# Five engines, ten hand-written orders: every table of a fused attention and expert kernel written anew

## The reference

```python
x = x + cluster_attention(_layernorm(x), ...)   # 8 batches of 512 rows
x = x + experts(_layernorm(x), ...)
x = x + landmark_attention(_layernorm(x), ...)
x = x + experts(_layernorm(x), ...)
```

```python
KV = K @ V
V = 0.25 * V @ (13.0 * I - KV @ (15.0 * I - KV @ (7.0 * I - KV)))
```

## Time and profile before

| | us |
|---|---|
| median of 3 runs | 1121.43 (1120.27 to 1126.33) |
| span of the profiled execution | 1121.9 |
| PE busy | 933.2 (83%) |
| VectorE busy | 831.1 (74%) |
| ScalarE busy | 641.6 (57%) |
| GpSimd busy | 472.3 (42%) |
| mean granted clock of TensorE | 0.925 of full speed |

### The profile page before, as it was taken

How to read it: one execution, slowest core, us unless ns; L and a number is a source line. 1 busy time by engine, 2 the same in 40 slices (tenths; PEclk the granted TensorE clock), 3 DMA queues, 4 the chain that set the end, 5 groups by cost and what they waited for, 6 DMA issues and landing times. The chain is left out here.

```text
span 1121.9 us, 37263 instructions
## 1 busy us (share of the span) xinstructions
PE 933.2 (83%) x15213; PEld 666.9 (59%) x15213; DVE 831.1 (74%) x2089; ACT 641.6 (57%) x1387; POOL 472.3 (42%) x443
## 2 busy tenths in 40 slices
PE   7899989998989888677888986597689989772898
PEld 5567667675766665456566665454466666552653
DVE  3899899888557996567776687878487898685556
ACT  2456656782664574456667585356376776382630
POOL 2355345227356630445524156512543454446421
PEclk8899989999999999888999998689789999895999
DMA  9700000002321100120101101100311110102533
GB/s 319 254 3 3 4 2 3 3 3 95 115 72 58 31 8 13 38 68 12 49 21 52 41 12 35 30 29 2 102 42 50 39 46 20 49 26 90 160 105 99
DMA packets 51079, 61.71 MB, mean 55 GB/s; under 512 B 5601, under 2 KB 46177, under 8 KB 50913
## 3 DMA queue, kind: packets, MB, share of 16 engines
q1 hardware_dynamic: 43584, 42.51, 11.8%
q0 software_dynamic: 5760, 15.74, 4.4%
q10 hardware_dynamic: 1568, 1.09, 0.3%
HBM read 29.70 MB, written 29.62 MB: 53 GB/s over the span
## 5 line engine op out<-in xcount | busy, mean ns | idle before, releaser
L764 POOL TENSOR_TENSOR a_pr<-a_pr,a_smax 128x512 f32<-128x512 f32 x128 | 133.3, 1042 | 177.5 <-DVE a_smax L877 168.0
L1267 POOL TENSOR_TENSOR b_tm<-b_aw,b_sq 128x640 f32<-128x640 f32 (+1 forms) x48 | 65.4, 1362 | 148.9 <-ACT b_sq L1505 143.5
L871 DVE TENSOR_TENSOR a_pr<-a_bank,a_mask 128x512 f32<-128x512 f32 x128 | 82.8, 682 | 42.0 <-PE a_bank L1066 34.7
L963 ACT ACTIVATE a_pr<-a_pr 128x512 f32<-128x512 f32 x128 | 78.6, 630 | 51.9 <-POOL a_pr L764 44.1
L1247 POOL TENSOR_TENSOR b_pa<-b_pa,b_amax 128x512 f32<-128x512 f32 x64 | 67.1, 1048 | 70.3 <-ACT b_pa L1470 61.8
L969 ACT ACTIVATE a_pT<-a_bank 128x512 f32<-128x512 f32 x128 | 71.1, 596 | 41.2 <-PE a_bank L1075 30.0
L1075 PE MATMUL a_bank<-ident,a_pr 128*128 128x128 f32 x512 | 76.4, 289 | 20.2 <-ACT a_pr L963 17.6
L1256 POOL TENSOR_TENSOR b_pa<-b_pa,b_asum 128x512 f32<-128x512 f32 x64 | 66.7, 1043 | 58.4 <-DVE b_asum L1371 54.2
L307 POOL DMA_INDIRECT rows_sorted<-f_rows,f_pos x60 | 58.2, 969 | 72.2 <-DVE f_pos L403 53.8
L1398 DVE SCALAR_TENSOR_TENSOR b_aw<-b_tm,b_inverse 128x320 f32<-128x320 f32 (+1 forms) x144 | 63.4, 440 | 33.1 <-PE b_inverse L1646 13.7
L318 POOL DMA_INDIRECT f_rows<-results_sorted,f_pos x60 | 58.6, 977 | 66.9 <-issue 34.4
(11 more groups left out here) (238 smaller groups left out, 2359.8 us busy)
## 6 DMA issues: line engine op xcount, KB each, us to landing
f_xg<-rows_sorted SPq DMA_DIRECT2D x42, 256.0 KB, 3.2
results_sorted<-f_yg SPq DMA_DIRECT2D x42, 256.0 KB, 2.3
rows_sorted<-f_yg SPq DMA_DIRECT2D x2, 2944.0 KB, 18.5
X<-in_x SPq DMA_DIRECT2D x7, 512.0 KB, 11.0
out<-X SPq DMA_DIRECT2D x7, 512.0 KB
experts_w<-in_e_wT SPq DMA_DIRECT2D x2, 1024.0 KB, 9.3
rows_sorted<-f_rows,f_pos POOLq DMA_INDIRECT x60
f_rows<-results_sorted,f_pos POOLq DMA_INDIRECT x60
```

What stands on the lines that cost most here:

```text
L764: nc.gpsimd.tensor_tensor(out=pr[:, u % AHEAD], in0=pr[:, u % AHEAD], in1=smax[:, u % AHEAD, :].unsqueeze(2).broadcast_to([P, HQ, KEYS]), ...
L871: pre.emptied(V_.tensor_tensor(out=pr[:, u % AHEAD], in0=gb[:].rearrange("p (h k) -> p h k", h=HQ), in1=mask[:, u // 4, :].unsqueeze(1).br ...
L963: nc.scalar.activation(pr[:, u % AHEAD], pr[:, u % AHEAD], ACT.Exp, scale=float(HD) ** -0.5)\
L1267: nc.gpsimd.tensor_tensor(out=tm[:, a:b, k], in0=aw3[:, a:b, k], in1=sq[:, a:b, k], op=ALU.subtract).then_inc(s_tm, 1)
```

## The change

All ten tables are replaced by others. On VectorE, ScalarE, GpSimd and SyncE each holds the same items as before in another order. On PE the 24 `idle` items are left out, in both blocks (546 items become 534, 705 become 693), and the rest is reordered. As `Ring` hands out banks by PE's table, an item may use another bank than before.

Nine waits are added in the bodies: `xn` of both blocks waits for what read or transposed the former batch, `v0`, `v1` and `vcl` of the cluster block for the former batch's `weigh`, `norm` for the `yT` two tiles back, `k0`, `k1` on ScalarE for the last scores two batches back, `v0`, `v1` on PE in both blocks for the transposed input, and `d` for the landmark sums. Each states a condition that the order of the items and the other waits implied before.

The diff, its code in full and of the tables the lines that are spoken of below:

```diff
@@ -795,6 +795,9 @@
                                 V_.bn_stats(stats[:, t, :], X[:, t, :]).then_inc(s_stats, 1)
                         dve.wait_ge(s_stats, b * NT)
                         layer_norm(nc, chain, stats, mean, rstd, scr, a * NT, b * NT)
+                    if n > 0:
+                        pre.filled_bank(dve, n - 1, "xT1")
+                        pre.filled_bank(dve, n - 1, "xb")
                     for t in range(NT):
                         tt = n * NT + t
                         V_.tensor_scalar(xn[:, t, :], X[:, bass.ds(tt, 1), :], mean[:, bass.ds(tt, 1)],
@@ -852,6 +855,7 @@
                         dve.wait_ge(s_vw, VW)
                         dve.wait_ge(s_zero, 1)
                     gb = pre.filled_bank(dve, n, item)
+                    wait_later(dve, s_pv, (n - 1) * UNITS)
                     for e in range(2):
                         r = slice(64 * e, 64 * e + 64)
                         last = V_.tensor_tensor(
@@ -881,6 +885,8 @@
                     t = int(item[4:])
                     dve.wait_ge(s_pv, n * UNITS + (4 * t + 4))
                     wait_later(dve, s_y, n * NT + (t - 1))
+                    if n * NT + t >= 2:
+                        pre.filled_bank(dve, (n * NT + t - 2) // NT, f"yT{(t - 2) % NT}")
                     o = O[:, 0:H * DV].rearrange("p (h d) -> p h d", d=DV)
                     V_.reciprocal(rsum[:, t % 2, :], o[:, :, HD:DV]).then_inc(s_rsum, 1)
                     dve.wait_ge(s_rsum, n * NT + (t + 1))
@@ -919,6 +925,8 @@
                     if n == 0:
                         act.wait_ge(s_rot, ROT)
                     pre.brought_out(act, n, [item])
+                    if n >= 2:
+                        pre.filled_bank(act, n - 2, f"score{UNITS - 1}")
                     for j in range(2):
                         nc.scalar.activation(keys[:, par, hh, j, 1:1 + T // GS, :],
                                              kT[:, hh, :].rearrange("p (g k) -> p g k", k=GS), ACT.Copy,
@@ -952,6 +960,7 @@
                     if n == 0:
                         act.wait_ge(s_zero, 1)
                     pre.brought_out(act, n, ["ckv"])
+                    wait_later(act, s_pv, (n - 1) * UNITS)
                     for e, r in ((0, 64), (1, 0)):
                         nc.scalar.activation(
                             V[e][r:r + 64, par, :, :, 0:HD],
@@ -1045,6 +1054,7 @@
                 elif item in ("v0", "v1"):
                     if n == 0:
                         pe.wait_ge(s_vw, VW)
+                    pre.brought_out(pe, n, ["xT0", "xT1"], item)
                     for t in (2 * int(item[1]), 2 * int(item[1]) + 1):
                         for kc in range(2):
                             last = mm(gb[:, (t % 2) * C:(t % 2 + 1) * C], xT[:, kc, t * P:(t + 1) * P],
@@ -1288,6 +1298,8 @@
                     elif n == B // 2 + 1:
                         experts.measured.wait(dve, ("m1", B * NT // 2 - 1))
                         layer_norm(nc, chain, stats, mean, rstd, scr, n * NT, B * NT)
+                    if n > 0:
+                        ring.filled_bank(dve, n - 1, "xT1")
                     for t in range(NT):
                         tt = n * NT + t
                         V.tensor_scalar(xn[:, t, :], X[:, bass.ds(tt, 1), :], mean[:, bass.ds(tt, 1)],
@@ -1540,6 +1552,7 @@
                         last = mm(gb[:], wq[:, kc, blk * P:(blk + 1) * P], xT[:, kc, :],
                                   start=(kc == 0), stop=(kc == 1))
                 elif item in ("v0", "v1"):
+                    ring.brought_out(pe, n, ["xT0", "xT1"], item)
                     for j in range(2):
                         t = 2 * int(item[1]) + j
                         for kc in range(2):
@@ -1552,6 +1565,7 @@
                     for hh in range(HH):
                         last = mm(gb[:, hh * M:(hh + 1) * M], bdQ[r, hh], klm[r, hh, :], start=True, stop=True)
                 elif item == "d":
+                    pe.wait_ge(s_k2, (n + 1) * 7)
                     if n == 0:
                         pe.wait_ge(weights.loaded, weights.all)
                     last = mm(gb[:], bones[:], k2n[:, par], start=True, stop=True)
@@ -1721,289 +1735,295 @@
 
 CLUSTER_ORDER = {
     "pe": """
-        0.idle0 0.idle1 1.idle0 0.xT0 0.xT1 1.idle1 0.lc 2.idle0 0.q0 0.k0 0.k1 0.wT 0.q1 0.xb 0.v0 0.xbT 0.ckv 0.v1
-        0.score0 2.idle1 3.idle0 0.turn0 0.turn1 0.turn2 0.weigh0 0.score4 0.weigh1 0.turn3 1.xT0 1.xT1 0.weigh2
-        0.weigh3 1.lc 1.q0 1.k0 0.turn4 0.turn5 0.turn6 0.yT0 0.score8 1.k1 1.wT 1.q1 0.turn7 0.weigh4 0.weigh5
...
+        0.xT0 0.xT1 0.lc 0.q0 0.wT 0.k0 0.xb 0.k1 0.xbT 0.q1 0.ckv 0.v0 0.v1 1.xT0 1.xT1 1.lc 0.score0 1.v0 1.wT 1.q0
+        0.turn0 1.k0 0.turn1 0.turn2 0.weigh0 0.turn3 0.score4 1.v1 1.q1 1.xb 1.k1 0.turn4 1.xbT 0.weigh1 0.turn5
...
     "dve": """
-        0.xn 0.lc 0.q0 0.k0 0.k1 0.lsum 0.q1 0.v0 0.ckv 0.v1 0.mask0 0.mask1 0.max0 0.max1 0.mask2 0.mask3 0.max2
...
+        0.xn 0.lc 0.lsum 0.q0 0.k0 1.xn 0.k1 0.v0 0.ckv 0.v1 0.q1 1.lc 1.lsum 0.mask0 0.max0 0.mask1 0.max1 0.mask2
...
 LANDMARK_ORDER = {
     "pe": """
-        0.idle0 0.xT0 0.xT1 0.q0 0.k0 m1.rx3.0 0.q1 m1.rx3.1 0.k1 0.v0 0.v1 0.S20 0.S21 0.S22 m1.lg3 0.S23 0.idle1
-        1.idle0 1.idle1 m1.lt3 2.idle0 0.sc0 0.kT 0.tc0 1.xT0 0.d 0.A 0.tc1 1.xT1 0.w0 0.w1 0.tc2 m1.s2 0.tc3 0.w2
...
-        2.ta7 3.N0.0 2.sv0 2.sv1 3.ta0 3.ta1 3.R1.0 3.ta2 3.N1.0 3.sa4 3.R2.0 2.pj0 2.pj1 3.N2.0 3.R3.0 3.N3.0
-        3.R4.0 3.N4.0 3.R5.0 3.ta3 3.ta4 3.ta5 2.pj2 3.ta6 3.N5.0 3.ta7 3.idle1 2.pj3 3.Z 3.sv0 3.sv1 3.pj0 3.pj1
-        3.pj2 4.xT0 3.pj3 4.xT1 4.q0 4.k0 4.q1 4.k1 m2.rx0.0 m2.rx0.1 m2.lg0 4.sc0 4.v0 4.tc0 4.v1 m2.lt0 m2.rx1.0
...
+        0.xT0 0.xT1 0.q0 0.q1 0.k0 m1.rx3.0 m1.rx3.1 0.k1 m1.lg3 0.v0 0.S20 0.v1 0.S21 0.S22 0.S23 m1.lt3 1.xT0 1.xT1
+        0.sc0 1.k0 1.q0 0.kT 0.tc0 0.tc1 0.d 0.w0 0.A 0.tc2 0.w1 m1.s2 0.tc3 0.w2 1.q1 0.w3 0.sc4 1.k1 0.tc4 0.tc5
...
+        3.ta3 2.pj3 3.N1.0 3.sa4 4.xT0 3.R2.0 3.N2.0 3.R3.0 3.ta4 4.xT1 3.N3.0 3.ta5 4.q0 3.ta6 4.k0 3.R4.0 3.ta7
+        4.k1 4.q1 3.N4.0 4.v0 4.v1 3.R5.0 4.sc0 4.S20 4.S21 3.N5.0 4.S22 4.tc0 4.tc1 4.S23 3.Z 4.w0 4.w1 4.tc2 4.tc3
+        3.sv0 3.sv1 4.sc4 3.pj0 3.pj1 3.pj2 3.pj3 4.w2 4.w3 4.tc4 4.tc5 4.kT 4.w4 4.tc6 4.sa0 m2.rx0.0 m2.rx0.1
...
     "dve": """
...
-        3.N0.0 3.na3 3.R1.0 3.U1.0 3.N1.0 3.sa4 3.R2.0 3.sa5 3.U2.0 3.sa6 3.sa7 3.N2.0 3.R3.0 3.U3.0 m1.co0 3.N3.0
-        2.pj0 2.pj1 m1.co1 3.R4.0 3.U4.0 m1.co2 m1.co3 3.N4.0 3.na4 3.na5 3.na6 3.na7 3.R5.0 3.U5.0 4.xn 3.N5.0
...
+        3.N0.0 m1.co2 2.pj0 2.pj1 3.R1.0 m1.co3 3.U1.0 2.pj2 4.xn 3.N1.0 3.sa4 3.sa5 3.R2.0 3.sa6 3.U2.0 3.sa7 3.na4
+        3.N2.0 3.na5 2.pj3 3.R3.0 3.U3.0 3.na6 3.na7 m1.co4 3.N3.0 m1.co5 4.q0 m1.co6 3.R4.0 4.k0 3.U4.0 m1.co7
+        m1.co8 m1.co9 3.N4.0 4.q1 4.k1 m1.co10 3.R5.0 m1.co11 3.U5.0 4.sc0 4.sc1 3.N5.0 4.sc2 4.sc3 4.S20 4.S21 4.S22
...
     "pool": """
-        m1.sc0 m1.sc1 m1.sc2 m1.sc3 m1.sc4 0.sa0 0.sa1 0.sa2 0.sa3 m1.sc5 0.na0 m1.sc6 m1.sc7 m1.sc8 m1.sc9 m1.sc10
-        m1.sc11 m1.sc12 m1.sc13 m1.sc14 m1.sc15 0.R0.0 0.na1 0.na2 0.sa4 0.R1.0 0.R2.0 0.sa5 0.sa6 0.sa7 0.na3 0.na4
...
-        2.R5.0 2.na7 3.na0 3.na1 3.sa3 3.R0.0 3.na2 m1.ga0 3.R1.0 m1.ga1 m1.ga2 3.na3 m1.ga3 3.R2.0 3.sa4 3.sa5
...
+        m1.sc0 m1.sc1 m1.sc2 m1.sc3 m1.sc4 m1.sc5 m1.sc6 m1.sc7 m1.sc8 m1.sc9 m1.sc10 m1.sc11 m1.sc12 m1.sc13 m1.sc14
+        0.R0.0 m1.sc15 0.sa0 0.sa1 0.sa2 0.sa3 0.na0 0.R1.0 0.na1 0.R2.0 0.na2 0.na3 0.R3.0 0.sa4 0.sa5 0.sa6 0.sa7
...
+        3.sa2 3.na0 3.sa3 3.na1 3.na2 2.R5.0 3.na3 m1.ga0 m1.ga1 m1.ga2 m1.ga3 3.R0.0 m1.ga4 m1.ga5 m1.ga6 m1.ga7
+        m1.ga8 3.R1.0 m1.ga9 3.sa4 3.R2.0 3.sa5 3.na4 3.sa6 3.sa7 3.na5 3.R3.0 3.na6 3.na7 m1.ga10 m1.ga11 m1.ga12
...
```

519 lines of the change are left out of this document (262 added, 257 removed).

## The result

The new tables take 1115.1 us against 1122.2 (medians of 20 runs each): a ratio of 0.9943, interval 0.9921 to 0.9966, so some 6 us less where 29 were forecast. The profiled execution spans 1112.9 us, 9.0 less than that of before.

What follows compares the result with a forecast made beforehand. TensorE, busy 933.2 of 1121.9 us, was taken as the bound, with 188.7 us idle plus lower-clock losses to win. Terms: 17 + 7 + 13 + 5 - 5 - 6 - 2 = 29, so 1093 us; range 1060 to 1130.

Steps and rivals of the forecast that it cites:

- Scatters: Router stages: second pass's sixteen scatters nearly together beside 20 us of PE work, gain 10; first pass loses 3; total gain 7.
- holes only move: Rival, no change: scatter bursts starve PE in three passes (loss 15) and gathers come late; about 1122 us, chance 0.12.
- VectorE in the cluster block: Cluster block: mask, max order costs VectorE time and cover for claims shrinks; the start wins about 4; net loss 5 us.
- tight score units: Rival, cluster block: a turn that comes before its exp stalls all PE work behind it; 1107 to 1132 us, chance 0.18.
- The hole: After the second expert pass: batch 4's earlier normalisation, projections, scores and softmax cover batch 3's last Newton steps; gain 17 us.
- third router: Stage 736.7 to 820.8 loses the batch 4 work that moved ahead, leaving less PE work between its items; loss 6 us.
- Newton steps elsewhere: Batches 0 to 2 and 4 to 6: more cover between N and R; three fifths of the lack counted; gain 13 us.
- Identity products: Both blocks: leaving out 24 PE items, about 16 us, most right ahead of waits; some eight count, gain 5 us.
- clock rival: Smaller gain: without identity products the clock at both blocks' starts falls to 0.80, costing 17 us; 1110 us, chance 0.07.
- The end: Kernel's end: all four output stores of PE's last item now follow VectorE's last adds; loss 2 us.
- The waits: Nine added waits, executed at most 153 times, name what earlier waits already imply; priced at 0, bounds 0 to -8 us.
- The third: Third sign of being wrong: the windows of the two blocks' starts show a clock below 0.85 (the products' part).

## Why the prediction was wrong

**Scatters** (gain 7). This is the step that failed. I counted TensorE's work beside the burst by its median times, "20 us of PE work beside them: gain 10", and it was of the kind that a burst of indirect steps draws out. The earlier trace rows had shown just that, single instructions of 0.3 us behind 1 us of "issue", and I had called it an affair of the third pass, "nothing and keep 10 either way". In the second pass the stage got 7.3 us longer instead of 10 shorter; with plain DMAs it is 5.8 shorter. "The sixteen nearly together" failed too: counted as I counted, from the logits' products, the sixteenth ends after 56 us (453.6 to 510.0) where it was 47, since it stands behind `0.R0.0`. TensorE did not wait for it at `m1.tt0`, so what this cost isn't shown. The rival "holes only move" named the starving in three passes and priced it at 15 us. That half of it held. Its other half, gathers that come late, did not: ten of the sixteen were issued by 700. It had a chance of 0.12, and its time was too high: 1122 as stated, and its own terms add up to 1124.

**VectorE in the cluster block** (loss 5, and 3 of the first pass). Measured 16.4 us in the profile, 1.4% with the landmark tables held old. With plain DMAs it is 6.4, so 10 us go with the indirect steps: in the new table `weigh` items, 32 small instructions each, lie beside the scatters and gathers of m0 (4.weigh12 takes 6.1 us there, 5.weigh0 3.7, and either took 0.45 before), where the old one had projections beside the scatters. TensorE in after, in 4.weigh12, the last of it with 4.weigh13 in the second row:

```profile
264.68 0.29 PE L1098 MATMUL a_bank<-a_V,a_pT 128*32 128x17 f32 x4 [1.14 <-issue]
266.11 0.68 PE L1098 MATMUL a_bank<-a_V,a_pT 128*32 128x17 f32 x33 [1.13 <-issue]
```

The reason that I gave did not show. The tight score units did not stall TensorE more (turns wait 10.2 us instead of 17.6), and writing the pairs back gained nothing. What does show is the 8.8 us behind 4.xn, which I had not looked at. The rival "tight score units" fell.

**The hole** (gain 17). Half right. Batch 4's first transposes came 25.4 us after the last products of the second pass (703.68 against 678.24; forecast 24), and 18 us more TensorE time passed in the stage up to batch 3's last projection, `3.pj3` (58.68 against 40.48). But it lasted 76.1 us, not 63.3. The sentence that failed is "Batch 3's chain itself is no shorter, so the stage ends when it did". It got longer: from the start of the stage to batch 3's `Z` 65.8 us pass (677.2 to 743.0) where it was 48.6 (673.8 to 722.4). Most of it, 12 us, came before batch 4's items could cover anything, up to the third R. Some 4 us of that passed before the first R, behind items that now stand ahead of it. Some 4 passed from R to N in the first two steps: ScalarE and VectorE took the first R's product, which TensorE had finished at 683.34, only at 686.18, while the gathers ran. And 4 went to the normalisation of batch 4 itself: VectorE's table has it ahead of its part of the second N, so that the third R waited for it. In after, TensorE, ScalarE and VectorE at the first R, then VectorE at the second N:

```profile
682.56 0.78 PE L1647 MATMUL b_inverse<-b_aw 64*64 64x80 f32 x32 [0.17 <-issue]
686.18 0.89 ACT L1510 ACTIVATE b_sq<-b_inverse 64x320 f32<-64x320 f32 x2 [2.96 <-remote]
686.18 0.49 DVE L1391 SCALAR_TENSOR_TENSOR b_uq<-b_aw,b_inverse 128x320 f32<-128x320 f32 x1 [2.11 <-remote]
...
703.12 1.38 DVE L1305 TENSOR_SCALAR b_xn<-X,norm_mean,norm_rstd 128x256 f32<-128x256 f32 x4
704.42 1.51 DVE L1410 SCALAR_TENSOR_TENSOR b_aw<-b_tm,b_inverse 128x320 f32<-128x320 f32 x3
```

TensorE had finished that N at 699.97. The last 5 us came under the cover. TensorE in after:

```profile
703.68 1.35 PE L1547 MATMUL b_bank<-ident,b_xn 128*128 128x128 f32 x4 [2.04 <-DVE b_xn L1305]
706.08 1.34 PE L1647 MATMUL b_inverse<-b_aw 64*64 64x80 f32 x32 [1.04 <-DVE b_aw L1410]
...
716.26 1.02 PE L1660 MATMUL b_inverse<-b_uq,b_sq 64*64 64x80 f32 x32
...
721.84 0.78 PE L1647 MATMUL b_inverse<-b_aw 64*64 64x80 f32 x32
...
728.15 0.78 PE L1660 MATMUL b_inverse<-b_uq,b_sq 64*64 64x80 f32 x32 [1.50 <-DVE b_uq L1400]
...
732.91 0.78 PE L1647 MATMUL b_inverse<-b_aw 64*64 64x80 f32 x32 [0.33 <-DVE b_aw L1410]
```

From N to R to N to R, 5.6, 6.3 and 4.8 us go by, where the old kernel took 4 to 4.4 (N at 707.34, the next R at 711.74). Batch 4's items between them are on VectorE's path too (62.86 us busy of 76.1, where it was 49.85 of 63.3). The cover was longer than the round trip, and the chain paid for it. With the third router behind it, whose loss of 6 I had set apart, the stretch to m2.tt0 is 5.4 us longer; with plain DMAs still 1.8. So 17 - 6 was wrong by some 16 us, and with plain DMAs by 13.

**Newton steps elsewhere** (gain 13). Right in kind and too small. The waits of N and R fell by 35 us, from 62.8 to 27.8, under the 45 set as the mark, and the two stretches that they fill are 20.3 and 11.7 us shorter. "Three fifths of a lack" undercounts: in the first stretch alone TensorE's idle time fell from 26.5 to 8.9 us.

**Identity products** (gain 5). In the new order this holds, so far as it can be told: putting them back takes 2 to 5 us (0.9960 and 0.9990 against 0.9943). It would have been wrong for the old order, in which leaving all of them out costs 1.5%, making them tiny 2.2% (17 and 25 us). The clock rival's price of 17 us is a fair one for the old tables. In the new ones the lower level does take more, by an estimate worked out as for the rival: (1 - 0.906) x 940.3 = 88 us of TensorE's time where it was (1 - 0.925) x 933.2 = 70. But with plain DMAs it also takes more, 47 us (0.948, 900.2) where it was 32 (0.964, 902.3), and putting products in doesn't win it back.

**The end** (loss 2). The stretch behind m3.tt0 is 10.0 us shorter, some 4 of them work that had been done earlier. The last router is 3.9 us longer. **The waits**, priced at nothing, cost nothing that can be told.

**The signs.** Of those for "right", the 24 us (25.4) and the 45 us of waits (27.8) came; the clock of the hole's stage stayed at 0.82, under 0.85, and the sixteen scatters took 33.7 us, not 30. Of those for "wrong", tight units did not come (the waits of turn and weigh named above sum to 28.3 us), and starved PE in the second pass did. The third came in part: of the two starts, the first has a clock of 1.00 and the landmark block's 0.78, but there it is 0.94 with plain DMAs, without any identity product, so it isn't the products' part alone.

With the indirect DMAs gone the new tables lead by 33 us, near the forecast 29. That is partly luck: hole and third router gave some 13 us less than their terms, the stretches of the Newton steps 34 where 13 were forecast, or 18 with the products' 5. What made the time miss the forecast by 22 us went away with the indirect DMAs. It stood in the rows as gaps inside TensorE's items, and I had priced it for one place only; that the other engines are held up as well I had not seen.

The Trainium skill ("DMA: Bandwidth & Descriptors", SWDGE vs HWDGE vs iDMA) says that descriptors of plain and indirect DMAs from GpSimd are made by software on that engine alike. The runs here tell them apart: 35.2 us of gaps beside the indirect ones, 1.4 beside the plain ones. The Trainium skill ("Runtime: NRT & Kernel Launch", Instruction fetch mechanics) says that the fetch of instructions is mostly hidden behind their issue. That the gaps are such a fetch no run here shows; in after the only queue that moved anything from 481 to 499 us, while the gaps ran, was that of the scatters (581 packets), and none of instructions did.

## What to carry to other kernels

Time worked out from an engine's own durations is only as good as its neighbours: before a burst of GpSimd's indirect DMAs is drawn together, look at what the other engines have beside it. Few, wide instructions fared better there than many small ones, though no run here tried that by itself. A chain that gets cover gets longer as soon as the cover exceeds its round trip on any of its engines, or as soon as what brings the cover (here batch 4's normalisation) stands ahead of the chain's own steps, so count the chain's new length and not only the work that fits in. A table that holds ten microseconds of one engine in a row needs ten microseconds of the others that don't ask for it; moved by ten items, the wait only moved.

## What the runs showed of the hardware

- A run of indirect DMA steps on GpSimd let TensorE issue one to four small instructions per 0.7 to 1.4 us, and held ScalarE up for 8.8 us, with a full bank waiting. An eighth of the bytes left 29.3 of 35.2 us of such gaps and a quarter of the rows 42.3; a plain DMA of the same bytes from the same queue left 1.4. Idle times put down to "remote" sum to 56.2 us on ScalarE and 61.6 on VectorE, and to none with plain DMAs.
- Beside wide products the same burst did little to TensorE: it was busy 11.55 of 14 us in the old kernel while ten scatters ran.
- Products without a use can pay or not, in the same kernel: 24 of them moved the clock from 0.910 to 0.933 and the time by 1.5 to 2.2% in the old order; in the new one they moved it from 0.909 to 0.919 (medians of the runs) and the time no lower.
